# An attention and linear-attention block on one core: values and sums of exponentials accumulated as the transposed operand of the output projection

## What is computed

```python
q, k, v = (qkv[:, :, 0], qkv[:, :, 1], qkv[:, :, 2])
q = rmsnorm(q, q_norm_w)
k = rmsnorm(k, k_norm_w)
...
attn = jnp.einsum('bnhd,bmhd->bhnm', q, k) * scale
attn = jax.nn.softmax(attn, axis=-1)
o = jnp.einsum('bhnm,bmhd->bnhd', attn, v).reshape(B, N, C)
o = o @ proj_w.T + proj_b
x = x + g_msa * o
h2 = modulate(rmsnorm(x, norm2_w), sh_mlp, sc_mlp)
ff = jax.nn.silu(h2 @ w1.T) * (h2 @ w3.T) @ w2.T
x = x + g_mlp * ff
```

## Time and profile before

| | us |
|---|---|
| median of three runs | 277.94 (277.62 to 278.91) |
| span of the profiled execution, first to last instruction | 274.4 |
| TensorE matmuls busy | 214.6 (78%) |
| VectorE busy | 220.0 (80%) |
| ScalarE busy | 169.7 (62%) |
| POOL busy | 158.6 (58%) |

### The profile page before, as it was taken

The page is one execution under the profiler, slowest core; times in us unless marked ns, Lnnn a source line. Parts: engine busy times, 40 slices in busy tenths (PEclk is TensorE's granted clock), DMA queues, the critical chain, the costliest instruction groups (busy, mean ns, idle before and its releaser), DMA issues. The chain is left out here.

```text
span 274.4 us, 7061 instructions
## 1 busy us (share of the span) xinstructions
PE 214.6 (78%) x2028; PEld 162.0 (59%) x2028; DVE 220.0 (80%) x700; ACT 169.7 (62%) x437; POOL 158.6 (58%) x431
## 2 busy tenths in 40 slices
PE   3406196998999989889899999599994899756763
PEld 2403053777677767767677777488882588533531
DVE  7495979899999999999999962587888899946322
ACT  0526235789898989889898875324340377654661
POOL 6184778888888887778887500011207486785300
PEclk9999565699999999999999999979999799995555
DMA  7710000000000000000000000000000000000112
GB/s 147 207 36 0 2 0 0 4 2 0 4 4 4 0 0 0 0 0 0 0 4 0 2 2 1 1 4 0 0 0 0 0 4 1 2 0 0 39 38 76
DMA packets 9554, 4.01 MB, mean 15 GB/s; under 512 B 2669, under 2 KB 9530, under 8 KB 9530
## 3 DMA queue, kind: packets, MB, share of 16 engines
q1 hardware_dynamic: 4170, 2.18, 2.9%
q10 hardware_dynamic: 5360, 1.54, 2.4%
HBM read 2.67 MB, written 1.05 MB: 14 GB/s over the span
## 5 line engine op out<-in xcount | busy, mean ns | idle before, releaser
L1268 DVE TENSOR_REDUCE nmax<-bank 128x4 f32<-128x512 f32 x64 | 42.6, 682 | 2.5 <-PE bank L1468 2.0
L1062 ACT ACTIVATE probs<-bank 128x512 f32<-128x512 f32 x64 | 37.6, 603 | 4.4 <-PE bank L1454 4.3
L1453 PE MATMUL bank<-qT,kT 128*128 128x128 bf16 x256 | 34.6, 222 | 0.3
L1454 PE MATMUL bank<-mT,sel 128*128 128x128 bf16 x256 | 34.5, 222 | 0.0
L1453 PEld LDWEIGHTS bank<-qT,kT 128*128 128x128 bf16 x256 | 25.4, 100 | 4.0 <-ACT mT L1095 1.3
L1454 PEld LDWEIGHTS bank<-mT,sel 128*128 128x128 bf16 x256 | 25.5, 99 | 2.8 <-issue 2.5
L1468 PE MATMUL bank<-kT,qT 128*128 128x256 bf16 x128 | 25.4, 282 | 0.6 <-DVE nmax L1268 0.6
L430 POOL TENSOR_TENSOR xs<-x,rstd 128x256 f32<-128x256 f32 x8 | 4.8, 612 | 32.6 <-DVE rstd L396 19.0
L543 ACT ACTIVATE th<-bank 128x256 f32<-128x256 f32 x24 | 9.2, 384 | 21.0 <-PE bank L776 11.1
L1498 PE MATMUL bank<-identb,parts 128*128 128x128 bf16 x256 | 20.8, 228 | 1.5 <-DVE kT L1350 0.9
L1498 PEld LDWEIGHTS bank<-identb,parts 128*128 128x128 bf16 x256 | 17.5, 104 | 5.2 <-DVE parts L1291 2.5
(11 more groups left out here) (247 smaller groups left out, 683.0 us busy)
## 6 DMA issues: line engine op xcount, KB each, us to landing
out_dram<-res SPq DMA_DIRECT2D x4, 256.0 KB, 2.3
xin<-in_x_dram ACTq DMA_DIRECT2D x1, 768.0 KB, 8.3
ada_n<-in_L_cond_ada_w_dram ACTq DMA_DIRECT2D x1, 384.0 KB, 3.7
xin<-in_x_dram ACTq DMA_DIRECT2D x1, 256.0 KB, 4.1
w_n<-in_L_cond_w_dram SPq DMA_DIRECT2D x2, 128.0 KB
qkv_n<-in_L_cond_qkv_w_dram SPq DMA_DIRECT2D x1, 192.0 KB, 4.5
w_n<-in_L_cond_w_dram SPq DMA_DIRECT2D x1, 170.5 KB
emb_n<-in_L_cond_emb_W_dram SPq DMA_DIRECT2D x1, 128.0 KB
```

Source lines behind the costliest of these rows:

```text
L1062: q.activation(probs[c][:, :, :].rearrange("p h t -> p (h t)"), bank[E_BANK[c % 2]][:, :], ACT.Exp, scale=SCALE).then_inc(s_p, 1)
L1268: q.tensor_reduce(nmax[q1][:, c * HPC:(c + 1) * HPC], bank[S_BANK[c % 2]][:, :].rearrange("p (h t) -> p h t", t=T), X_AXIS, ALU.max, negat ...
L1453: q.matmul(dst, kT[q0][:, h // 2, h % 2, :], qT[q0][:, h // 2, :], start=True, stop=False)
L1454: last = q.matmul(dst, sel[:, h, :], mT[q0][:, :], start=False, stop=True)
```

## The change

The values get a new layout, so that the four chunks can be added up in one region of 128 columns: in a matmul of chunk c the 8 value columns stand at 8 x c of the 32 output rows and zeros elsewhere. The four chunks accumulate, and the region ends up as 128 rows, one for each feature of a head, in the order (i, c, d) with head 4c + i. A second tensor `vone`, laid out alike with ones in place of values, gives in another region of 128 columns the sum of exponentials, repeated for the eight features of its head. VectorE takes the reciprocal of the 128 x 128 sums (`rden`) and multiplies, and the product is `oT` at once. The weights of the projection are put into the same order by one copy on ScalarE (`proj_p`) ahead of their transpose. Gone are `oT4` and its copy, four transposes, `rsum`, `o` with its transpose, and the copy into `oT`.

```diff
+VROW = HPC * (VW + DH)
-        vpad = [sb(f"vpad{p}", [128, H, VW]) for p in range(2)]
-        oT4 = sb("oT4", [128, NC * T])
-        rsum = sb("rsum", [128, H])
-        o = sb("o", [128, H, DH])
+        vpad = [sb(f"vpad{p}", [128, NC, VROW]) for p in range(2)]
+        vone = sb("vone", [128, VROW])
+        rden = sb("rden", [128, T])
...
+                a.wait_ge(ld_proj, 16)
+                q.activation(proj_p[:, :].rearrange("p (i c d) -> p i c d", c=NC, d=DH),
+                             proj_n[:, :].rearrange("p (c i d) -> p i c d", i=HPC, d=DH), ACT.Copy).then_inc(pv_a, 1)
...
-                if is_seq(t - 1):
-                    b = t - 1
-                    a.wait_ge(s_oTp, b + 1)
-                    wait(a, s_proj, b)
-                    q.activation(oT[:, :], bank[P_BANK][:, 0:T], ACT.Copy).then_inc(s_oT, 1)
...
-                if is_seq(t):
-                    b = t
-                    a.wait_ge(s_o, NC * b + NC)
-                    wait(a, s_oq, b)
-                    q.activation(oT4[:, :], bank[O_BANK][:, :], ACT.Copy).then_inc(s_oT4, 1)
...
+            q.memset(vone[:, :], 0.0).then_inc(seeded, 1)
...
+            q.memset(vone[:, :].rearrange("p (j w) -> p j w", w=VW + DH)[:, :, 0:DH], 1.0).then_inc(seeded, 1)
...
-                    q.tensor_scalar(vpad[q0][:, :, 0:DH], vall[:, bass.ds(b, 1), :].rearrange("p a (h d) -> p (a h) d", d=DH),
+                    q.tensor_scalar(vpad[q0][:, :, :].rearrange("p i (c w) -> p i c w", w=VW + DH)[:, :, :, 0:DH],
+                                    vall[:, bass.ds(b, 1), :].rearrange("p a (c i d) -> p (a i) c d", i=HPC, d=DH),
                                     1.0, None, ALU.mult).then_inc(s_vpad, 1)
                 if is_seq(t - 1):
                     b = t - 1
-                    v.wait_ge(s_oq, b + 1)
-                    oq = bank[O_BANK][:, :].rearrange("p (h w) -> p h w", w=VW)
-                    q.reciprocal(rsum[:, :], oq[:, :, DH:DH + 1].rearrange("p h a -> p (h a)")).then_inc(s_rec, 1)
+                    v.wait_ge(s_o, NC * b + NC)
+                    q.reciprocal(rden[:, :], bank[O_BANK][:, T:2 * T]).then_inc(s_rec, 1)
                 cut(1)
                 if is_seq(t - 1):
                     b = t - 1
                     v.wait_ge(s_rec, b + 1)
-                    wait(v, s_oTp, b)
-                    q.tensor_tensor(o[:, :, :], bank[O_BANK][:, :].rearrange("p (h w) -> p h w", w=VW)[:, :, 0:DH],
-                                    rsum[:, :].unsqueeze(2).to_broadcast([128, H, DH]), ALU.mult).then_inc(s_on, 1)
+                    wait(v, s_proj, b)
+                    q.tensor_tensor(oT[:, :], bank[O_BANK][:, 0:T], rden[:, :], ALU.mult).then_inc(s_oT, 1)
...
-                        wait(e, s_on, t)
+                        wait(e, s_oT, t)
                     e.wait_ge(s_p, NC * t + c + 1)
+                    slot = slice(c * VW, (c + 1) * VW)
                     for i in range(HPC):
-                        last = q.matmul(bank[O_BANK][VW * i:VW * (i + 1), c * T:(c + 1) * T], vpad[q0][:, c * HPC + i, :],
-                                        probs[c][:, i, :], start=True, stop=True)
+                        q.matmul(bank[O_BANK][VW * i:VW * (i + 1), 0:T], vpad[q0][:, i, slot], probs[c][:, i, :],
+                                 start=c == 0, stop=c == NC - 1, skip_group_check=True)
+                    for i in range(HPC):
+                        last = q.matmul(bank[O_BANK][VW * i:VW * (i + 1), T:2 * T], vone[:, slot], probs[c][:, i, :],
+                                        start=False, stop=c == NC - 1, skip_group_check=True)
                     last.then_inc(s_o, 1)
...
-                if is_seq(t - 1):
-                    b = t - 1
-                    e.wait_ge(s_oT4, b + 1)
-                    for i in range(NC):
-                        last = q.transpose(bank[O_BANK][:, i * T:(i + 1) * T], oT4[:, i * T:(i + 1) * T], ident[:, :])
-                    last.then_inc(s_oq, 1)
...
-                if is_seq(t - 1):
-                    b = t - 1
-                    e.wait_ge(s_on, b + 1)
-                    wait(e, s_x1, b)
-                    q.transpose(bank[P_BANK][:, 0:T], o[:, :, :].rearrange("p h d -> p (h d)"), ident[:, :]).then_inc(s_oTp, 1)
```

More of the change, by code:

```diff
@@ L152, in dit_then_linear_attention @@
         proj_n = sb("proj_n", [128, D])
+        proj_p = sb("proj_p", [128, D])
         w1_n = sb("w1_n", [128, FC, D])
@@ L302, in dit_then_linear_attention @@
         s_o = sem("s_o")
-        s_oT4 = sem("s_oT4")
-        s_oq = sem("s_oq")
         s_rec = sem("s_rec")
-        s_on = sem("s_on")
-        s_oTp = sem("s_oTp")
         s_oT = sem("s_oT")
@@ L376, in dit_then_linear_attention @@
         P_COND, P_ADA, P_QKV, P_MOD, P_MODS, P_PAR, P_W1, P_W3, P_W2, P_BIAS = range(1, 11)
-        A_SQUARE, A_SIN, A_QKV, A_SQUARES, A_TANH, A_DONE = 1, 2, 3, 4, 5, 10
+        A_SQUARE, A_SIN, A_QKV, A_SQUARES, A_TANH, A_PROJ, A_DONE = 1, 2, 3, 4, 5, 6, 11
         V_COND, V_ADA, V_ANG, V_MOD, V_RSTD, V_RSTDS, V_MODS, V_LIN, V_DONE = 2, 4, 12, 15, 28, 41, 50, 54, 60
@@ L1175, in _ @@
                 q.memset(vpad[p][:, :, :], 0.0).then_inc(seeded, 1)
+            q.memset(vone[:, :], 0.0).then_inc(seeded, 1)
             q.memset(mparts[:, :].bitcast(F32), 0.0).then_inc(seeded, 1)
-            v.wait_ge(seeded, 3)
-            for p in range(2):
-                q.memset(vpad[p][:, :, DH:DH + 1], 1.0).then_inc(seeded, 1)
+            v.wait_ge(seeded, 4)
+            q.memset(vone[:, :].rearrange("p (j w) -> p j w", w=VW + DH)[:, :, 0:DH], 1.0).then_inc(seeded, 1)
             v.wait_ge(pt, P_COND)
@@ L1422, in prepare_weights @@
                     q.transpose(bank[2][:, c * 128:c * 128 + 128], w2_n[:, c * 128:c * 128 + 128], ident[:, :])
-                e.wait_ge(ld_proj, 16)
-                q.transpose(bank[2][:, FC * 128:FC * 128 + 128], proj_n[:, :], ident[:, :]).then_inc(pt, 1)
+                e.wait_ge(pv_a, A_PROJ)
+                q.transpose(bank[2][:, FC * 128:FC * 128 + 128],
+                            proj_p[:, :], ident[:, :]).then_inc(pt, 1)
                 e.wait_ge(seeded, 5)
@@ L1536, in step @@
                     e.wait_ge(s_oT, b + 1)
+                    wait(e, s_x1, b)
                     q.matmul(bank[P_BANK][:, 0:T], projT[:, :], oT[:, :], start=True, stop=True).then_inc(s_proj, 1)
```

## The result

The changed kernel takes 281.09 us (median of eight runs, 279.21 to 282.19), the kernel before 277.65 (eight runs, 276.58 to 278.91): 1.0123 times as long, 95% interval 1.0095 to 1.0151. That is slower, as forecast, but by 3.4 us and not by 8. The profiled execution took 280.77 us with a span of 279.0.

The account below looks back on a forecast made before the run. VectorE was taken as the bound, its late operations running into POOL's chain. Eleven steps 6.0, two steps 1.4 and the last three 0.6 gave +8.0: span 282.4, time 286.0 us; range 281 to 293 for 8 in 10.

Parts of the forecast that it names:

- Eleven steps at +0.55: 6.0 us: Steady attention steps: each goes from 7.75 to 8.30 us, part of the reciprocal's added time being given back; 6.0 us in all.
- The reciprocal, +0.89: VectorE's reciprocal, grown from 128x16 to 128x128: 1.13 us in place of 0.24 each step; bounds +0.69 and +1.11.
- Late operations come free: VectorE's small operations late in the step: moved later, they meet an idle POOL, so the step grows +0.55, not +0.89.
- L993 still runs to 7.53 and holds L1305 up, as now: Late in the step: POOL's last operation ends 7.53 us after L1311's end and still delays VectorE's L1305, 0.50 us now.
- the bound +0.22: Lower bound of a steady step's growth: +0.22 us if L1305 also comes free, taking 0.18 us in place of 0.50.
- The step before, 7.75: Length of a steady step in the kernel before, from the starts of twelve reciprocals: 85.3/11 = 7.75 us.
- The last intervals, +0.8, +0.6 and 0.2 each: Steps after 143.1 us: the first two cost +0.8 and +0.6 us, the last three, where VectorE waits for TensorE, +0.2 each.
- about even: TensorE's work in a step: sixteen more matmuls, +0.83 us, against lost transposes of 0.60 and 0.32 us and a lost wait.
- The chain through TensorE, close under the step: Path through TensorE's values and the transpose of pr: 8.22 us against a step of 8.30, so it adds nothing.
- ScalarE's gain is hidden: ScalarE loses two copies, 0.88 us a step, but no VectorE operation waits on it there, so nothing shows.
- The span against the time: The profiled execution's span of 274.4 us lies 3.5 us under the median of 277.94; that part was left unchanged.
- a reciprocal of 0.69 with full relief: Case of a reciprocal adding only 0.69 us with late operations fully relieved: 280 to 283 us, chance 0.10.

Follow-up runs that it names:

- a_turn_early: The changed kernel with TensorE's transpose of pr moved ahead of the last of the four chunks of values and sums; 281.26 us, 1.0127 of the kernel before.
- a_narrow: The changed kernel with the reciprocal cut to 128x16 and spread over the multiply by a broadcast, most normalization left out; 275.22 us, 0.9882 of the kernel before.
- b_again: The kernel before, unchanged, run again for a second profile; 278.33 us, ratio 0.9998 to the kernel before.

## Why the prediction was right and wrong

The sign was right, and 281.09 us lies just inside the range, at its low end. The forecast itself, 286.0, was 4.9 us too high: +8.0 was forecast and +3.4 measured. The step that failed is the term "Eleven steps at +0.55: 6.0 us": it measured +1.9 us against one profile of the kernel before and +0.5 to +0.8 against the other, 0.05 to 0.20 a step. The end was mis-sized the other way, about 1.8 us forecast for four intervals that took 3.2; with the end as forecast the time would have been near 279.7, under the range, so that it lies inside is luck.

For the reading of L1305 one line of the kernel before is needed beside the earlier trace rows:

```profile
101.30 0.89 POOL L989 TENSOR_TENSOR partner<-qk,rope 128x96 f32<-128x96 f32 x2
```

By its steps:

- *The reciprocal, +0.89:* it measured +0.70, almost the lower bound of +0.69 from 16 to 32 elements. The point of 2 elements carried a start-up share, which I had argued away; the larger rows were nearer to the size asked for. 0.19 a step, 2.1 us over eleven.
- *Late operations come free:* L1307, L1311 and L1363 do, as said, L1311 in every step. What failed is "L993 still runs to 7.53 and holds L1305 up, as now": L993 doesn't hold L1305 in the kernel before either. There L1305 (101.30 to 101.80) is over before L993 starts (102.26), and what is under way is the first of the two L989. L993 starts 6.96 us after L1311's end, so by the rows L1305, moved to 6.89, would come just ahead of it. So it does: the seed (now L1295) slips into the gap and takes 0.17 us. I had named this case as the bound +0.22 and set it aside on the ground that POOL's chain would have to shorten as much. With it (0.33 less) and the measured reciprocal (0.19 less), the same sum is 8.30 - 0.52 = 7.78, and with 0.11 for the cast L1347 (L1358 before: median 186 ns, now 293) 7.89: measured 7.93 and 7.95.
- *The step before, 7.75:* this term was taken for a property of the kernel, and is one execution's mixture of steps of 7.6 and 8.0. The earlier trace rows showed both kinds and I read them only as a spread of durations. Against the second profile's 7.88 the change costs 0.05 to 0.08 a step.
- *The last intervals, +0.8, +0.6 and 0.2 each:* from 143.1 us in the kernel before on, the four took +0.75, +0.76, +1.18 and +0.47, 3.2 us where these terms give about 1.8. The first two were right; in the third the added matmuls come in full (+0.85, forecast +0.83 as their length), and 0.33 us more stand ahead of them. I had priced TensorE as "about even" although it is busy 14.42 of 15 us there: the removed transposes do not stand on the path on which the added matmuls stand. So the end, to which I gave 2.0 of 8.0 us, costs more than the eleven steps.
- *The chain through TensorE, close under the step:* the wait of L1356 for L1531 is there (0.16 us in the step shown, 0.6 in the ten), and removing it in a_turn_early gave nothing. The chain adds nothing to the steady step, as said.
- *ScalarE's gain is hidden:* its share fell by five points, as said. By a_narrow's times the change without the wide reciprocal is worth about 1%, so something of the removals shows; whether it is ScalarE's share, and through which wait, stays open.
- *The span against the time:* I put 3.5 us around the span. It is about 2 (278.93 us in all for b_again's span of 276.9); the profiled execution of before was a short one, not one with more around it. The sum, made from it, was added to the median, and so inherited a base with more short steps than b_again has.
- Of the rivals, none came. The case "a reciprocal of 0.69 with full relief", 280 to 283 us, chance 0.10, is nearest to what happened in the steps; its time was met with the help of an end that it did not foresee.

## What to carry to other kernels

Where two engines release each other once a step, work on one shows up only as far as it lengthens the other's wait: count that wait per step rather than busy shares, and look whether the step before is one length or a mixture of two. Price the end of such a pipeline by itself, each added instruction against the engine that is the bound there: here its intervals repeated to 0.01 us in two profiles of each kernel, and in one of them TensorE's added matmuls counted in full and VectorE's longer reciprocal not at all. Before you write that one operation holds another up, look whether the two overlap in the timeline. For an operand larger than any in the trace, the slope between the two largest sizes was the right one here.

## What the runs showed of the hardware

- Reciprocal on VectorE: 107 ns for 2 elements a partition, 245 for 16, 344 for 32, 944 for 128. From 16 on that is 6.2 ns an element. The repeat count of 8 in the Trainium skill (VectorE: DVE Perf Modes, "First, the fixed hardware budget"), from which I had estimated 8.3, is not borne out as a time per element; the measurement decides.
- The small late operations of 0.17 to 0.18 us take up to 0.56 (L1311 in the earlier trace rows) when a POOL operation is under way, and end with it; the reciprocal, which reads PSUM, stays at 937 to 958 ns in every step of every run that has it at 128 elements. The rule of the Trainium skill (SBUF — State Buffer, "Who interferes with whom"), that VectorE and GpSimd exclude each other only over a shared pair of ports, agrees with these rows; the profile counts the time held as busy.
- Added work can be nearly free: 0.7 to 0.8 us more on an engine shown busy 75.57 of 77.50 us cost 0.05 to 0.2 us a step.
- One kernel had executions with spans of 274.4 and 276.9 us at the same work: 1.4 us of it by how many of eleven steps were short or long, 1.2 us ahead of the first reciprocal.
- Float32 matmuls of 32 output rows, four side by side: a group of eight records starts about 0.22 us after the one before (163.59, 163.81, 164.02 in after, accumulating). Without accumulation four such groups are through in 1.10 us; with one of them at 0.40 us, as in after, I estimate (1.10 - 0.40)/3 = 0.23 from start to start.
